# An expert-routed layer: the last round of GpSimd's row loop, and how the program's block ends

## What is computed

```python
x, cond_2048 = ...           # (8, 512, 1024), (8, 1024): the 8 taps of a filter
L0_cond_b = ...              # (1024,)
w_router, w_experts = ...    # (8, 1024), (8, 1024, 1024)

def _L0_cond_ref(x, w, b):   # depthwise causal convolution with 8 taps over the sequence
    y = jax.lax.conv_general_dilated(x, w, window_strides=(1,), padding=[(K - 1, 0)], feature_group_count=D, ...)
    return y + b

def _L0_ffn_ref(x, w_router, w_experts):
    logits = jnp.einsum('bsh,eh->bse', x, w_router)
    idx = jnp.argmax(logits, axis=-1)
    all_out = jnp.einsum('bsh,efh->bsef', x, w_experts)
    return jnp.take_along_axis(all_out, idx[:, :, None, None], axis=2)[:, :, 0, :]

x + _L0_ffn_ref(_L0_cond_ref(x, cond_2048[:, None, :], L0_cond_b), w_router, w_experts)
```

## Time and profile before

| what | value |
|---|---|
| median of three runs | 570.39 us (569.82 to 573.39) |
| profiled execution, its own time | 571.02 us |
| its span | 569.4 us |
| PE busy with matmuls | 531.6 us, 93% of the span |
| DVE, ACT, POOL busy | 345.7, 192.5, 183.9 us |
| mean granted TensorE clock | 0.975 |

### The profile page before, as it was taken

How to read it: one execution, slowest core, us unless ns; L and a number is a source line. 1 busy time by engine, 2 the same in 40 slices (tenths; PEclk the granted TensorE clock), 3 DMA queues, 4 the chain that set the end, 5 groups by cost and what they waited for, 6 DMA issues and landing times.

```text
span 569.4 us, 10165 instructions
## 1 busy us (share of the span) xinstructions
PE 531.6 (93%) x3151; PEld 448.4 (79%) x3152; DVE 345.7 (61%) x389; ACT 192.5 (34%) x361; POOL 183.9 (32%) x198
## 2 busy tenths in 40 slices
PE   8999999999699999998999999999999999999920
PEld 6988888798588888886788888888888888888810
DVE  7999999985295834248874342583276234827520
ACT  7773654745640111035361010430061001606100
POOL 1420650635335313431222442303340433124320
PEclk9999999999999999999899999999999999999975
DMA  8895575939788597649979646496669645884551
GB/s 344 313 387 179 189 303 185 337 88 366 224 295 299 161 350 230 194 149 352 385 235 367 180 148 199 134 341 188 184 194 348 188 122 165 271 257 153 167 160 37
DMA packets 54695, 133.42 MB, mean 234 GB/s; under 512 B 7184, under 2 KB 27792, under 8 KB 54416
## 3 DMA queue, kind: packets, MB, share of 16 engines
q0 software_dynamic: 17376, 59.10, 29.1%
q1 hardware_dynamic: 15840, 54.42, 27.2%
q10 hardware_dynamic: 21456, 19.60, 13.6%
HBM read 93.44 MB, written 39.65 MB: 234 GB/s over the span
## 4 chain that ended last, share of the span: by engine, by line
PE 65%; DMA 3%; issue 2%; ACT 1%; DVE 1%; POOL 1%; ACTq 1%; SPq 0%; POOLq 0%; DVEq 0%
PE ps L1069 64%; DMA y_sorted<-rows_even,pos_i 2%; ACT w_sb L515 1%; DMA out<-x_row,idx 1%; POOL y_sorted L1121 1%; DMA y_blk<-y_sorted 1%; DVE w_sb L813 0%; DVE y_cols L828 0%; PE ps L965 0%; ACTq L356 0%; SPq L356 0%; DVE x_row L841 0%; PE ps L978 0%; ACT ys L534 0%; ACT w_sb L523 0%
## 5 line engine op out<-in xcount | busy, mean ns | idle before, releaser
L1069 PE MATMUL ps<-w_sb,ys 128*128 128x512 f32 x1680 | 383.7, 391 | 2.7 <-DVE w_sb L813 2.7
L1069 PEld LDWEIGHTS ps<-w_sb,ys 128*128 128x128 f32 x1680 | 316.4, 189 | 69.1 <-DVE w_sb L813 3.1
L828 DVE STREAM_TRANSPOSE y_cols<-y_blk 128x1024 f32<-128x1024 f32 x37 | 46.0, 1244 | 165.0 <-PE ps L1069 141.6
L534 ACT CAST ys<-y_cols 128x1024 fp32r<-128x1024 f32 x37 | 39.0, 1055 | 274.0 <-DVE y_cols L828 266.5
L676 DVE SCALAR_TENSOR_TENSOR y_pre<-x_all,cst,y_pre 128x1024 f32<-128x1024 f32 x72 | 87.2, 1276 | 0.1
L813 DVE TENSOR_TENSOR w_sb<-w_raw,w_sb 128x1024 fp32r<-128x1024 f32 x56 | 64.2, 1220 | 20.4 <-ACT w_sb L515 20.4
L945 PE MATMUL ps<-x_all,bands 128*128 128x128 f32 x640 | 76.3, 277 | 0.2
L945 PEld LDWEIGHTS ps<-x_all,bands 128*128 128x128 f32 x640 | 72.9, 192 | 2.8 <-issue 2.8
L515 ACT CAST w_sb<-w_raw 128x1024 fp32r<-128x1024 f32 x56 | 54.0, 1050 | 21.6 <-PE ps L1069 12.3
L1180 POOL COPY idx<-idx_in_sb 128x1 int32<-128x1 int32 x34 | 11.5, 339 | 152.8 <-DMA out<-x_row,idx 145.7
L1156 POOL DMA_INDIRECT out<-x_row,idx x32 | 36.8, 1152 | 72.3 <-DVE x_row L841 66.1
(11 more groups left out here) (113 smaller groups left out, 188.9 us busy)
## 6 DMA issues: line engine op xcount, KB each, us to landing
w_raw<-experts SPq DMA_DIRECT2D x56, 512.0 KB, 3.6
y_blk<-y_sorted ACTq DMA_DIRECT2D x148, 128.0 KB
x_all<-x_t SPq DMA_DIRECT2D x32, 520.0 KB, 5.5
y_sorted<-rows_odd POOLq DMA_DIRECT2D x8, 520.0 KB, 11.0
w_lead<-experts SPq DMA_DIRECT2D x8, 512.0 KB, 4.2
bands<-conv_full SPq DMA_DIRECT2D x2, 1024.0 KB, 10.2
y_blk<-y_sorted SPq DMA_DIRECT2D x8, 128.0 KB
idx_in_sb<-y_sorted POOLq DMA_DIRECT2D x36, 1.0 KB
```

Of the source, the lines that this page charges most:

```text
L828: V.transpose(y_cols[k][:, :, :].rearrange("p m (t i) -> p t m i", t=4), y_blk[:, k, :, :, :]).then_inc(y_blocks, 1)
L1069: mm = nc.tensor.matmul(out_ps[k][:, f * HALF:(f + 1) * HALF], ys[:, a, k, c, :], w_sb[:, (b * HC + c) * H + f * HALF:(b * HC + c) * H + ( ...
```

## The change

`take_ids`, `gather_x` and `load_ids`, with the wait for the landed scatter ahead of them, become one function `get_next`. The loop's body is written out instead of being a Python loop over two slots. The second `get_next` of a round now stands in an `If(i < last)`, and ahead of the round's second scatter there is a wait for `row_out[0]`. The waits behind the loop follow: one transfer of token numbers fewer for buffer 0, and a wait for the last gather into buffer 1, which nobody waited for before. The block is opened with `no_gpsimd_drain=True`.

```diff
-        block = ctx.enter_context(nc.Block())
+        block = ctx.enter_context(nc.Block(no_gpsimd_drain=True))
...
+            def get_next(t, k, nth_of_ring, looked):
+
+
+                pool.wait_ge(row_out[k], nth_of_ring * 16)
+                take_ids(k, nth_of_ring, looked)
+                gather_x(k, idx[:, k:k + 1])
+                load_ids(t + RING, k)
...
             with pool.Fori(0, ROUNDS) as i:
                 with pool.If(i < last + 1):
-                    for k in range(RING):
-                        t = i * RING + (LOOP + k)
-                        o = (LOOP + k + 1) % RING
-                        if k:
-                            scatter(t - 1, o, idx[:, o:o + 1])
-
-                        pool.wait_ge(row_out[o], (i + 2) * 16)
-                        take_ids(o, i + 2, i * RING + (k + 3))
-                        gather_x(o, idx[:, o:o + 1])
-                        load_ids(t + 3, o)
+                    get_next(i * RING + (LOOP + 1), (LOOP + 1) % RING, i + 2, i * RING + 3)
+                    scatter(i * RING + LOOP, LOOP % RING, idx[:, LOOP % RING:LOOP % RING + 1])
+                    with pool.If(i < last):
+                        get_next(i * RING + (LOOP + 2), LOOP % RING, i + 2, i * RING + 4)
                     with pool.If(i < full):
+
+                        pool.wait_ge(row_out[LOOP % RING], (i + 2) * 16)
                         scatter(i * RING + (LOOP + 1), (LOOP + 1) % RING, idx[:, (LOOP + 1) % RING:(LOOP + 1) % RING + 1])
 
             pool.wait_ge(idx_in[FIRST % RING], (last + 3) * 16)
-            pool.wait_ge(idx_in[LOOP % RING], (last + 3) * 16)
+            pool.wait_ge(idx_in[LOOP % RING], (last + 2) * 16)
             pool.wait_ge(y_got[(LOOP + 3) % RING], (last + ((LOOP + 3) // RING + 1)) * 64)
             pool.wait_ge(y_got[(LOOP + 4) % RING], (last + ((LOOP + 4) // RING + 1)) * 64)
+            pool.wait_ge(x_got[(LOOP + 1) % RING], (last + 3) * 16)
             pool.wait_ge(third_out, 16)
```

## The result

The changed kernel took 554.41 us (median of 4 runs, 552.58 to 557.83) against 570.74 us for the kernel before beside it (4 runs, 569.82 to 573.39). The ratio is 0.9726, with a 95% interval of 0.9695 to 0.9757: 14 to 17 us less. The profiled execution took 552.58 us at a span of 550.9.

What follows compares the result with a forecast made beforehand. The prediction took PE's unbroken matmuls, then a tail of 16.2 us behind the last scatter's landing, as the bound; 6.3 + 9.3 + 0 = 15.6 us off 570.39 gave 554.8 us, range 553.2 to 562.0.

Steps and rivals of the forecast that it cites:

- Where the time is: Whole kernel: changes before PE's end at 544.7 count only if PE waits; whatever is saved behind it counts in full.
- The fetch behind the last scatter: Last round on POOL: copy, gather and load for slots that do not exist go, 6.3 us less.
- the 0.2 allowed: Behind the last scatter's landing: 0.2 us for a register operation and the branch to the block's end.
- The DRAIN: POOL at the block's end: leaving its DRAIN out saves 9.3 us, taken from bounds of 0 and 9.3.
- A: Rival: the DRAIN's work is owed and paid behind the program; chance 0.10 in full, 0.07 in part.
- B: Rival at the program's end: dropping the last fetch brings nothing, only the DRAIN goes; 561.1 us, chance 0.04.
- C: Rival: branches stall POOL's loop beyond its cover; 8.0 us a round eats the gain, 10 gives 603 us; chance 0.02.
- The loop, cost 0: POOL's loop: added branches and wait take 0.1 to 0.2 us a round, hidden under PE's work, so cost 0.
- cover: In the loop: the time POOL's turn of 7.5 us leaves free against PE's 10.96, put at 3.5 us a slot.
- both parts in full: Program's end: last fetch and DRAIN both save their whole time, 6.3 and 9.3 us; the likeliest case, chance 0.76.
- A in part: Rival: some of the DRAIN's work is paid behind the program; 556 to 563 us, chance 0.07.
- A in full: Rival: all the DRAIN's work is paid behind the program, time falls only 6.3 us to 564.1; chance 0.10.

Runs made afterwards that it cites:

- e2: The changed kernel with POOL's DRAIN put back at the block's end, so only the last fetch is gone; 563.09 us.
- e1: The kernel before with POOL's DRAIN at the block's end left out and nothing else changed; 560.23 us.
- e4: The kernel before with two more POOL DRAINs, one ahead of its loop and one behind the final waits; 567.34 us.
- e5: The changed kernel with the block's DRAIN kept and one more POOL DRAIN in each round of the loop, behind the wait for the landed scatter; 556.80 us.
- e7: The changed kernel with a POOL memset of 128 x 3072 f32 as filler ahead of each copy of token numbers; 587.26 us.
- e8: The changed kernel with a POOL memset of 128 x 6144 f32 as filler ahead of each copy of token numbers; 650.13 us.
- e9: The changed kernel measured and profiled again without any edit, beside e10; 555.45 us.
- e3: The changed kernel with one explicit POOL DRAIN right behind its loop, while the last scatter is still under way; 559.17 us.
- e10: The changed kernel without the last round's other work for slots that do not exist, on POOL, ACT and DVE; 551.29 us.
- e6: The kernel before with one more POOL DRAIN at the point where 35 of its 151 transfers are issued; 573.12 us.

## Why the prediction was right

- *Where the time is.* It said that behind PE's end everything counts in full and before it nothing does. The tail fell by 15.7 us with a sum of 15.6, and PE's stretch did not change beyond what executions of one kernel differ by.
- *The fetch behind the last scatter, 6.3 us.* Measured alone, 6.6 us of the tail (e2), 6.3 to the branch: 553.2 to 559.7 before, which is 6.5, and 550.3 to 550.5 in e2, the 0.2 allowed. The other 0.3 are the DRAIN's 0.16 and a landing 0.14 us sooner. The wait left is that for the landing, as said.
- *The DRAIN, 9.3 us.* Measured alone, 10.0 us of the tail (e1), of which 9.3 are the DRAIN; the rest is mostly that this execution's last scatter landed in 4.6 us instead of 5.05. Taking the upper bound was right, since the work shows nowhere in the measured time. The rows of before could not decide that between 0 and 9.3; e1 did. The 183 ns, which the prediction took for a DRAIN with nothing to do, are not that price: it is 46 ns (e4). That its length hangs on what POOL has issued was right too, and it is now 82 ns a transfer.
- *Rivals.* A (paid behind the program) would leave e1 at 570 us: 560.23, and time less span stayed at 1.6 to 1.7 us in e1, e2 and the changed kernel. (It is 1.9 to 2.0 in e4 and e5, with the DRAIN, and in e7 and e8, without it.) B (the turn brings nothing) would leave e2 at 570: 563.09. C (a slower loop) did not occur: the added branch took 39 ns in the median, PE shows no pause.
- *The loop, cost 0.* Right, with a cover that was put too large: 3.5 us a slot for one of 2 to 2.5. The 0.2 us a round lie far inside either. Rival C's threshold of 8 us a round would have been nearer to 5 or 6.
- *The chances.* What the prediction lists as faster (both parts in full, B, A in part, half of A in full) adds up to 0.92, not to its 0.89. Its range of 553.2 to 562.0 holds the result either way.
- *The profiled run.* The prediction's span was 553.8, the profile showed 550.9. The 2.9 us are PE's earlier end, 542.0 for 544.7, and not the change; the runs' median, 554.41, has no such luck in it, and e9's was 555.45.
- *A rule weighed against a row.* The Trainium skill, "VectorE: DVE Perf Modes", section "The DRAIN you can't avoid", has the runtime's DRAINs at about 12 ns on all engines. Taken as the price of this one it would have left 6.3 us of the gain; e1 alone shows 10. The row decided rightly. This DRAIN stands in the kernel's own block. There the trace is near the 12 ns for SP, ACT and DVE alone (7, 8 and 17 ns): PE's took 2,273 ns, which the prediction left out, and ended with PE's last matmul, so it cost nothing.

## What to carry to other kernels

Look at what lies between the last matmul and the end of the span, instruction by instruction, with the sequencers' lines: shares of busy time show none of it. A DRAIN of GpSimd at a block's end cost 82 ns here for each transfer (of 128 rows) that GpSimd had issued since the last one, less the oldest 38 or so of a long program. So a program with many can leave it out, with every transfer waited for by its semaphore, or spread it over the loop where GpSimd waits anyway. In a loop that fetches ahead, ask in the last round for each instruction whether its slot exists, on all engines and not only the one where it showed.

## What had not been expected

- The DRAIN's price is linear in the count of transfers, down to 46 ns with none, whatever their bytes: a round's 6 (two scatters and two gathers of 512 KB, two loads of 1 KB) cost 6 x 82.5 ns, and the first 35, with eight plain and 24 indexed writes of 520 KB, 82.3 ns each. It works while the last transfer is still under way, if that lands before the work is done (e3).
- The last scatter of 512 KB landed in 5.0 us beside ACT's four loads of 128 KB and POOL's gather, in 3.8 us beside POOL's gather and load (e7, e8), and in 3.3 us alone (e10).
- A program of 151 transfers pays for 112 at its end, and a DRAIN at the 35th does not change that (e6).
